# Five steps of the attention stage played at other heads: input statistics, input normalisation, rotary products, feed-forward transposes and router

## What is computed

```python
x = x + _layernorm(_L0_attn_ref(_layernorm(x), ...))
x = x + _layernorm(_L0_ffn_ref(_layernorm(x), ...))

# _L0_attn_ref
ct_q = _lin(x, w_down_q, b_down_q)
q = (_lin(ct_q, w_up_q, b_up_q) + _rope(_lin(ct_q, wq_r, bq_r), cos, sin)).reshape(bs, sl, nh, hd)
ct_kv = _lin(x, w_down_kv, b_down_kv)
k = (_lin(ct_kv, w_up_k, b_up_k) + _rope(_lin(ct_kv, wk_r, bk_r), cos, sin)).reshape(bs, sl, nh, hd)
v = _lin(ct_kv, w_up_v, b_up_v).reshape(bs, sl, nh, hd)
scores = jnp.einsum('bqhd,bkhd->bhqk', q, k) / np.sqrt(hd)
a = jnp.einsum('bhqk,bkhd->bqhd', jax.nn.softmax(scores, axis=-1), v).reshape(bs, sl, nh * hd)
return _lin(a, wo, bo)

# _L0_ffn_ref: 8 experts of width 512, one of them for each token
logits = x @ router_w.T
# scores: the sigmoid of the largest logit at its expert, 0 elsewhere
gate, up = jnp.split(jnp.einsum('eth,ehf->etf', x * scores, gate_up_proj), 2, axis=-1)
routed = jnp.einsum('etf,efh->eth', up * jax.nn.silu(gate), down_proj).sum(axis=0)
shared = jax.nn.silu(x @ shared_gate_w) * (x @ shared_up_w) @ shared_down_w
return shared + routed
```

## Time and profile before

| what | us |
|---|---|
| median of 3 runs | 484.71 |
| lowest and highest | 484.57, 486.15 |
| the profiled execution | 486.15 |
| its span, first to last instruction | 484.3 |
| TensorE busy | 443.0 (91%) |
| VectorE busy | 253.3 (52%) |
| ScalarE busy | 184.9 (38%) |
| GpSimd busy | 133.9 (28%) |

### The profile page before, as it was taken

One profiled execution on the slowest core, in us unless ns is written; L12 is line 12 of the kernel. 1 busy time (PEld: TensorE's weight loads), 2 busy tenths in 40 slices (PEclk: granted clock), 3 DMA queues, 4 the chain that ended last, 5 costly groups with the idle time before them and its releaser, 6 DMA issues.

```text
span 484.3 us, 7950 instructions
## 1 busy us (share of the span) xinstructions
PE 443.0 (91%) x2597; PEld 284.7 (59%) x2598; DVE 253.3 (52%) x591; ACT 184.9 (38%) x383; POOL 133.9 (28%) x195
## 2 busy tenths in 40 slices
PE   7888889999999997979899999999999999999691
PEld 6545556676767663644566655666666666655451
DVE  4455567968787767758659312222222222234775
ACT  2406557585858574554321221222222222221010
POOL 1214234343434343034020102111111110058533
PEclk9999899999999998999899999999999999999996
DMA  9762236363636364410747001111111111123311
GB/s 255 169 76 72 73 88 187 96 197 89 201 92 192 99 198 103 145 46 23 240 173 240 21 12 34 43 51 46 45 53 43 43 43 45 43 89 108 110 43 65
DMA packets 53990, 48.35 MB, mean 100 GB/s; under 512 B 5862, under 2 KB 49638, under 8 KB 53958
## 3 DMA queue, kind: packets, MB, share of 16 engines
q1 hardware_dynamic: 47424, 39.23, 28.1%
q0 software_dynamic: 1872, 5.11, 3.9%
q10 hardware_dynamic: 4662, 3.59, 2.6%
HBM read 25.78 MB, written 9.31 MB: 72 GB/s over the span
## 4 chain that ended last, share of the span: by engine, by line
PE 62%; DVE 14%; POOL 8%; issue 6%; DMA 3%; SPq 2%; ACT 2%; ACTq 0%; POOLq 0%; DVEq 0%
PE bank L1209 41%; PE bank L1213 8%; PE bank L1360 3%; PE bank L1308 3%; PE bank L1344 3%; DVE nmax L947 2%; SPq L435 2%; POOL pv L638 2%; PE bank L1284 2%; DMA stacks<-parts_q 2%; POOL x_sb L588 2%; DVE wall L977 1%; DMA x_sb<-x 1%; DVE stats_at L880 1%; POOL rstd_at L536 1%
## 5 line engine op out<-in xcount | busy, mean ns | idle before, releaser
L1209 PE MATMUL bank<-wall,stacks 128*128 (+2 forms) x616 | 213.0, 489 | 6.5 <-DVE stacks L1142 6.0
L1209 PEld LDWEIGHTS bank<-wall,stacks 128*128 128x128 f32 x616 | 111.5, 191 | 69.5 <-issue 59.6
L947 DVE TENSOR_REDUCE nmax<-bank 128x2 f32<-128x512 f32 x128 | 84.8, 686 | 46.1 <-PE bank L1308 45.9
L1138 DVE TENSOR_TENSOR stacks<-stacks,bank 128x512 f32<-128x512 f32 x39 | 26.8, 686 | 85.2 <-PE bank L1209 85.2
L1308 PE MATMUL bank<-stacks 96*128 96x256 bf16 x256 | 48.1, 274 | 10.4 <-DVE nmax L947 7.3
L622 POOL DMA_INDIRECT stacks<-x_sc,row_i x23 | 22.0, 957 | 124.2 <-PE bank L1213 124.2
L822 ACT ACTIVATE stacks<-bank 128x512 f32<-128x512 f32 x39 | 23.3, 597 | 81.6 <-PE bank L1209 78.1
L1142 DVE COPY stacks<-bank 128x512 f32<-128x512 f32 x39 | 26.9, 690 | 48.1 <-PE bank L1213 47.8
L784 ACT ACTIVATE pv<-bank 128x512 f32<-128x512 f32 x64 | 38.3, 604 | 34.8 <-PE bank L1360 34.0
L1360 PE MATMUL bank<-stacks 99*128 99x256 bf16 x256 | 49.5, 276 | 1.2 <-ACT wall L784 1.1
L784 ACT ACTIVATE wall<-bank 128x512 f32<-128x512 f32 x64 | 38.4, 606 | 25.8 <-PE bank L1360 24.8
(11 more groups left out here) (154 smaller groups left out, 530.4 us busy)
## 6 DMA issues: line engine op xcount, KB each, us to landing
wall<-gate_up SPq DMA_DIRECT2D x8, 1024.0 KB, 5.2
stacks<-parts_k SPq DMA_DIRECT2D x96, 64.0 KB, 2.6
stacks<-parts_q SPq DMA_DIRECT2D x91, 64.0 KB, 2.6
wall<-down SPq DMA_DIRECT2D x8, 512.0 KB, 6.5
y_exp<-stacks ACTq DMA_DIRECT2D x23, 128.0 KB, 1.7
x_tok<-wall SPq DMA_DIRECT2D x8, 256.0 KB, 2.6
stacks<-x_tok SPq DMA_DIRECT2D x16, 128.0 KB
out<-stacks SPq DMA_DIRECT2D x8, 256.0 KB, 2.2
```

Source lines behind the costliest of these rows:

```text
L947: dve.tensor_reduce(nmax[:, half, qt, 2 * pair:2 * pair + 2], two(sm_bank[u % 2]), AX.X, ALU.max, negate=True).then_inc(sm["sm_max"], 1)
L1138: dve.tensor_tensor(hid, sg, fu[:, :], ALU.mult).then_inc(sm["h_sb"], 1)
L1209: last = pe.matmul(out_ap, lhsT, rhs, start=(n == 0), stop=(n == len(pairs) - 1))
```

## The change

Only the tables `order` of three engines differ. No instruction is added or taken away.

```diff
 # GpSimd
-            order = {0: ("M1",), 2: ("B_power",), 8: ("A_kres", "M0",),
+            order = {0: ("M1",), 6: ("B_power",), 8: ("A_kres", "M0",),
...
 # VectorE
-            order = {0: ("E_xn2",), 1: ("A_T",), 2: ("B_stats",), 3: ("B_norm",), 5: ("E_router",),
-                     6: ("D_div0",), 8: ("D_div1",), 9: ("N_v",), 11: ("D_y",),
+            order = {0: ("E_xn2",), 1: ("A_T",), 5: ("E_router", "B_stats",),
+                     6: ("D_div0",), 8: ("D_div1", "B_norm",), 9: ("N_v",), 11: ("D_y",),
...
 # TensorE
-            order = {0: ("A_R",), 1: ("A_Q",), 2: ("M1", "A_QK",), 3: ("E_xn2T",), 5: ("E_router",),
+            order = {0: ("A_R",), 1: ("A_Q",), 2: ("M1", "E_xn2T",), 3: ("A_QK",), 4: ("E_router",),
```

## The result

| | before | changed |
|---|---|---|
| median, us | 485.07 (484.57 to 486.15, 4 runs) | 492.13 (489.28 to 494.87, 4 runs) |
| the profiled execution | 486.15, span 484.3 | 493.12, span 491.3 |
| mean granted clock of it | 0.981 | 0.985 |

The ratio is 1.0161, with a 95% interval of 1.012 to 1.0201: slower by 7.1 us, where 6.5 us were forecast. The same kernel once more, beside later experiments, took 491.33 us (489.5 to 494.05, 6 runs) against 484.94, ratio 1.0145 [1.0115, 1.0175]. Over all 37 executions of it on record the median is 493.3 us (489.28 to 497.24), so the four of the table lie a little low. Ratios here are estimated from single executions, without those in the chip's slower state, and so differ a little from the quotient of the two medians beside them.

What follows compares the result with a forecast made beforehand. TensorE was taken to set the pace, busy 23.09 of a slot's 23.70 us. Added waits 0.78 + 0.54 + 2.80 + 1.29 + 0.83 + 0.25 = 6.49 us on the median 484.71 gave 491.2 us, range 488.3 to 493.2.

Steps and rivals of the forecast that it cites:

- E_xn2T, slots 2 to 5: Behind M1 at head 2, a 0.52 us wait for ScalarE's copy of M1 replaces the rotary wait: +0.78 us.
- E_xn2T, slot 6: Behind M1, with no A_QK there, E_xn2T waits for the copy of M1: +0.54 us.
- E_router, slots 2 to 6: At D_avT0, no longer covered by the router, a 0.56 us wait for the logits copy in five slots: +2.80 us.
- B_stats at D_avT1: Behind the logits on VectorE, B_stats leaves D_avT1 at its old start, 150.73, with no slack left: no cost.
- B_norm, slots 2 to 4: Behind the second division on VectorE, B_norm makes B_xnT wait 0.43 us in all per slot: +1.29 us.
- slot 1: No E steps, so VectorE runs behind; D_avT1 +0.40 us, and B_xnT waits for B_norm: +0.83 us in all.
- slot 0: B_xnT waits for B_norm, but TensorE waits for GpSimd later; bounds 0 and 0.83, taken as +0.25 us.
- The block fits in: Rival: VectorE's steps overlap more, so the 1.29, 0.83 and 0.25 fall away: 488.8 us; chance 0.12.
- Faster: Rival: the wait for the rotary rows simply goes, with bank 7 free in time: 483.4 us; chance 0.05.
- Taken up later: Rival: added waits are absorbed later, needing shrunken waits at heads 13 to 15: about 485.5 us; chance 0.04.
- The clock: Rival: one to three more half-clock stretches, 492.8 to 496.0 us, chance 0.12; slot 6's stretch gone, 489.6, chance 0.05.

Runs made afterwards that it cites:

- only_xn2t: Kernel before with only A_QK and E_xn2T changing places on TensorE: 487.34 us against 485.6, ratio 1.0015 [0.9985, 1.0045].
- only_stats: Kernel before with only B_stats, B_norm (VectorE) and B_power (GpSimd) moved to heads 5, 8 and 6: 487.05 us, ratio 1.0022 [0.9994, 1.005].
- both: Changed kernel with M1 and its copy at head 1 and VectorE's copy of the logits at head 4: 488.11 us, 3.2 less than the changed kernel.
- qk_again: Repeat of the kernel before with A_QK alone moved to head 3, ahead of E_xn2T: 484.87 us against 485.7, ratio 0.9985 [0.9962, 1.0009].
- the three single parts: Kernel before with one part each: A_QK and E_xn2T exchanged, 487.34 us; E_router at head 4 on TensorE, 488.82; B steps moved, 487.05.
- three_undone: Changed kernel with M1 and its copy at head 1, logits copy at head 4, B steps at their old heads: 484.34 us against 485.7, ratio 0.9975.
- qk_at_3: Kernel before with A_QK alone moved from head 2 to head 3, ahead of E_xn2T: 484.63 us against 485.6, ratio 0.9982 [0.9951, 1.0012].
- m1_at_1: Changed kernel with M1 and its copy one head earlier, at head 1: 489.4 us, 1.9 less than the changed kernel.
- copy_at_4: Changed kernel with VectorE's copy of the logits one head earlier, behind the maxima of head 4: 490.05 us, 1.3 less than the changed kernel.

## Why the prediction was right

The forecast was 6.5 us with three waits at three named places; it measured 7.1, and 6.4 in the repeat. The interval of the first ratio reaches from 5.8 to 9.8 us, so that the medians came so near is partly luck. What bears the forecast out is the terms, from the checkpoints:

| term | forecast | measured |
|---|---|---|
| E_xn2T, slots 2 to 5 | 0.78 | 1.17 (only_xn2t) |
| E_xn2T, slot 6 | 0.54 | 0.56 (its wait) |
| E_router, slots 2 to 6 | 2.80 | 5 x 0.61 = 3.05 |
| B_stats at D_avT1 | 0 | 0.00 (only_stats) |
| B_norm, slots 2 to 4 | 1.29 | 3 x 0.41 = 1.23 |
| slot 1 | 0.83 | 0.75 |
| slot 0 | 0.25 | none that shows |
| sum | 6.49 | 6.76 |

The 7.00 between the two profiled executions has other things in it that come to some 0.2 together: the transfer at slot 4's end 0.31, the opening loads 0.80, slot 0 -0.59, one stretch at half clock for another about -0.1 (below), and -0.2 that slots 2 to 4 made up behind head 10.

*E_xn2T.* The mechanism was right, the size a third low. The step that was off is the spacing of 0.06 us from a releaser to the waiting engine. It was read from L914 to L1284, and holds there and from L958 to D_avT1 (152.38 + 0.42 = 152.80 to 152.86). For L767 to E_xn2T it was 0.14: 145.73 + 0.36 = 146.09 to 146.23. In four slots that is 0.32 of the 0.39 missing.

*E_router.* Five waits, as forecast, for the same reason too small: L1002 ended at 152.40 and D_avT0 started at 152.54, 0.14 again, which turns 0.56 into 0.64 against 0.61 measured.

*B_stats and B_norm.* D_avT1 kept its distance from D_avT0 to 0.01 us and B_xnT waited 0.41 where 0.43 was worked out. The working held D_avT0 at its old place, "without the delays above", and added the delays afterwards. That adding was allowed, since only_stats with D_avT0 on time and the changed kernel with D_avT0 waiting show the same 0.41: in both, VectorE starts its block right behind the copy of the logits that D_avT0 follows. It doesn't hold where they part: in "both" the copy is a head earlier, and B_stats costs 0.52 at D_avT1. The text had not argued this.

*Slot 1 and slot 0.* Slot 1 had D_avT1 0.41 later (forecast 0.40) and lost 0.75. In slot 0 B_xnT did wait 0.68 for B_norm, but three heads later TensorE waits for GpSimd anyway. From head 0 to head 0, slot 0 took 29.69 to 29.99 in the six traces without the block on VectorE, and 29.11 to 29.78 in the six with it. The lower bound, nothing, was the right value as far as these can tell.

*The rivals.* "The block fits in" fell: in all six traces with the block (five kernels and the repeat) the last transposes waited. "Faster" would have needed the copy of M1 to end at M1's own end, and even with ScalarE idle it only starts 0.32 behind M1's start and takes 0.37. "Taken up later" fell too: behind head 10 slots 2 to 5 took as long as before within 0.1, and slot 1 0.15 less, apart from the transfer. "The clock" was half right: the stretch at 190 us went, but one at 214 us came in both traces of the changed kernel. The first had cost what it was priced at, about 1.6: M1 to M0 of slot 6 took 15.47 before and 14.08 in qk_again at full clock, 0.18 of that a longer wait for maxima which qk_again had there. The second cost 1.47. The rule cited there from the Trainium skill (TensorE: Matmul & The Clock Gate, Part 1), that the throttled clock is the default and activity releases it, by which more waiting would bring more such stretches, isn't borne out by their count from 36 us on, without the last, which runs to the end of every trace: three in the trace of before, two in the changed kernel's and three in its repeat. In slots 2 to 4, where the waits were added, no trace shows less than the full clock.

What I had not foreseen is the transfer of M1's rows at the head 0 behind slot 4, 0.31 us. It appeared, at one head 0 or another, in the repeat, the three single parts and three_undone as well (0.2 to 0.5 us in all), and in none of before, qk_at_3, qk_again, m1_at_1, copy_at_4 and both. No experiment was made on it, and its cause stays open.

## What to carry to other kernels

When a step is moved away from a wait on an engine that plays in order, ask what buffer the step that takes its place writes and who has yet to read it: here two steps that had waited for next to nothing came to stand where the one shared bank was still full. A step that only sits between two others can be the cover of a third engine's work, and its move costs that cover, though it waits for nothing itself. And a wait that is removed in one place is a gain only up to the next engine that was running late: sum the checkpoints of a slot, not the waits.

## What the runs showed of the hardware

The spacing from a releaser's end to the waiting TensorE instruction was 0.06 us for L914 and L958, and 0.14 to 0.15 for L767 and L1002 (m1_at_1: 146.34 to 146.49). The kind of wait doesn't make the difference: L1308, which waits for the maxima to empty its bank, started 0.06 behind them (L947) in each of 15 waits of before, and L1327, which waits for data of GpSimd, 0.05 to 0.06 behind L582 in some waits and 0.14 in others. What tells them apart in the records of all twelve traces is the number of semaphores. The instructions that waited for one started 0.05 to 0.06 behind the end of their releaser on VectorE, ScalarE or GpSimd, 347 times without exception. Of those that waited for two, as E_xn2T and D_avT0 do, 92 started 0.13 to 0.15 behind: all those in which the semaphore recorded first of the two came last. Where the other came last, as for L1308, it was 0.05 to 0.06 again. No experiment changed the number of semaphores of a step, so the reason stays open.

From 36 us on TensorE fell to half clock (1.2 of 2.4 GHz) two to four times in each trace, the stretch at its very end left out, and what such a stretch costs depends on what TensorE had to do. The one at 214 us in the changed kernel cost 1.47: M0 of slot 6 to the next M1 took 10.35 there and in the repeat, and 8.87 to 8.89 in the ten traces without it. The one at 190 us in the repeat cost 0.2: M0 of slot 5 to M1 of slot 6 took 7.92 against 7.76, and on to M0 of slot 6 15.09 against 15.05. TensorE was busy for 1.10 of those 2 us in the first trace, where the clock was full (the row of 190 to 192 us above), which would explain it: the slower work went into idle time. They come at different places in executions of one kernel, and over 37 executions of the changed kernel the time fell by about 3.0 us for each 0.01 of mean granted clock, which ran from 0.969 to 0.987. That is some 5.4 of the 8.0 us between the shortest and the longest, and it is why a part worth 1 us is read from a slot's checkpoints and not from a median of 12.
